# Two-layer cross-attention: the first layer's bias column computed for two batches at once, its averages over partitions in one rounded product of four columns

## What is computed

```python
q = Wq y + bq; k = Wk y + bk; v = Wv x + bv        # 1x1 convolutions over channels, 8 heads of 16 channels
scores = q k^T / sqrt(128)                          # per head, channel by channel: 16 x 16, summed over L = 1024
out = softmax(scores) v
o = Wo out + bo + x
o_hat = (o - mean(o)) * rsqrt(var(o) + 1e-5)        # mean and variance over channels and L of a batch
h = o_hat * gn_w + gn_b
```

## Time and profile before

| | |
|---|---|
| median of 3 runs | 1253.28 us |
| profiled execution, device time | 1253.11 us |
| its span | 1251.3 us |
| TensorE matmul busy | 1239.6 us, 99% |
| TensorE weight load busy | 968.7 us, 77% |
| VectorE busy | 843.2 us, 67% |
| ScalarE busy | 807.7 us, 65% |
| GpSimd busy | 295.0 us, 24% |

### The profile page before, as it was taken

The page is one execution under the profiler, slowest core; times in us unless marked ns, Lnnn a source line. Parts: engine busy times, 40 slices in busy tenths (PEclk is TensorE's granted clock), DMA queues, the critical chain, the costliest instruction groups (busy, mean ns, idle before and its releaser), DMA issues.

```text
span 1251.3 us, 24584 instructions
## 1 busy us (share of the span) xinstructions
PE 1239.6 (99%) x7860; PEld 968.7 (77%) x7860; DVE 843.2 (67%) x1953; ACT 807.7 (65%) x2884; POOL 295.0 (24%) x297
## 2 busy tenths in 40 slices
PE   8999999999999999999999999999999999999999
PEld 6788888888887888888878877677776767677677
DVE  6777777777747767767667776776665677766554
ACT  6676776666617887887577877655555577755441
POOL 4444443222233233233333305100000111000000
PEclk9999999999999999999999999999999999999999
DMA  9689899999755445554555559998788999888872
GB/s 329 230 289 290 284 289 336 308 309 311 271 189 167 152 152 175 178 172 152 169 166 181 177 177 333 284 270 239 234 243 236 270 255 257 234 225 244 235 222 85
DMA packets 196590, 291.49 MB, mean 233 GB/s; under 512 B 14160, under 2 KB 119888, under 8 KB 195760
## 3 DMA queue, kind: packets, MB, share of 16 engines
q1 hardware_dynamic: 196464, 289.92, 74.5%
HBM read 183.96 MB, written 105.91 MB: 232 GB/s over the span
## 4 chain that ended last, share of the span: by engine, by line
PE 93%; DVE 4%; issue 1%; DMA 1%; SPq 0%; ACT 0%; DVEq 0%
PE bank L695 28%; PE bank L728 23%; PE bank L573 14%; PE bank L759 5%; PE bank L812 5%; PE bank L795 5%; PE bank L645 3%; PE bank L558 2%; PE bank L663 2%; DMA lora_raw_q<-in_factors_q 1%; PE bank L678 1%; PE bank L600 1%; PE bank L617 1%; PE bank L547 1%; DVE op L1364 1%
## 5 line engine op out<-in xcount | busy, mean ns | idle before, releaser
L1032 ACT ACTIVATE bank<-bank,negs 128x128 f32<-128x128 f32 x1024 | 353.9, 360 | 119.4 <-DVE negs L1314 118.5
L695 PE MATMUL bank<-hT,wq 128*128 128x512 f32 x1488 | 363.8, 396 | 0.0
L728 PE MATMUL bank<-wo,op 128*128 128x512 f32 (+1 forms) x1356 | 346.1, 393 | 2.0 <-DVE h_blk L1408 1.5
L695 PEld LDWEIGHTS bank<-hT,wq 128*128 128x128 f32 x1488 | 273.4, 188 | 60.8
L728 PEld LDWEIGHTS bank<-wo,op 128*128 128x128 f32 x1356 | 252.0, 188 | 62.9 <-issue 6.2
L1053 ACT ACTIVATE probT<-bank 128x512 f32<-128x512 f32 x256 | 152.6, 606 | 169.1 <-PE bank L795 166.5
L1309 DVE TENSOR_REDUCE maxes<-bank 128x4 f32<-128x512 f32 x256 | 175.1, 684 | 94.0 <-PE bank L759 93.6
L1032 ACT ACTIVATION_READ_ACCUMULATOR bank<-bank,negs 128x1 f32 x1024 | 231.3, 226 | 0.0
L573 PE MATMUL bank<-wkv_hi,yT 128*128 128x512 f32 x512 | 198.1, 415 | 0.7 <-POOL wkv_lo L1579 0.5
L1408 DVE TENSOR_TENSOR h_blk<-bank,h_blk 128x512 f32<-128x512 f32 x111 | 76.3, 687 | 95.5 <-PE bank L728 94.6
L573 PEld LDWEIGHTS bank<-wkv_hi,yT 128*128 128x128 f32 x512 | 96.5, 188 | 19.3 <-issue 1.7
(11 more groups left out here) (148 smaller groups left out, 1659.5 us busy)
## 6 DMA issues: line engine op xcount, KB each, us to landing
q_dram<-q_part SPq DMA_DIRECT2D x96, 512.0 KB, 5.7
q_stack<-q_dram SPq DMA_DIRECT2D x128, 384.0 KB, 4.8
yT_in<-in_ctx_turned SPq DMA_DIRECT2D x32, 512.0 KB, 4.9
y_in<-in_ctx SPq DMA_DIRECT2D x32, 512.0 KB, 7.1
x_in<-in_x SPq DMA_DIRECT2D x32, 512.0 KB, 5.9
h_dram<-h_out SPq DMA_DIRECT2D x32, 512.0 KB, 7.4
h_in<-h_dram SPq DMA_DIRECT2D x32, 512.0 KB, 4.0
h_blk<-h_dram SPq DMA_DIRECT2D x64, 256.0 KB, 5.2
```

What stands on the lines that cost most here:

```text
L695: m = pe.matmul(bank(u % 2).rearrange("p (a n) -> p a n", a=2), wq[:, block, part, c, :], hT[(group + 1) % 2][:, :, of, c, :], start=c == ...
L728: mm = pe.matmul(place[:, columns], op_of(pair, m)[:, of, c, :], wo[m][w][:, c, columns], start=fresh and c == 0 and of == 0 and w == 0, s ...
L1032: act.activation(part, part, ACT.Exp, bias=negs[:, n % NEGS, j:j + 1], scale=SCORE1, accum_out=sums[:, score_column(k), g, j:j + 1]).then_ ...
```

## The change

The repeated value bias becomes a third 128-column block of `first` and its column goes. The product `n1^T bv` is computed as `Wo (att bv)`: VectorE multiplies `att` by the repeated bias and sums along the row (`weigh_bias`), giving one column of `att_bv` for each batch; in odd chunks one product `woT0` x two columns (`bias_product`, ahead of `kv` chunk 5) makes both, and one VectorE operation adds `bo` to both (`add_bias`, within `partition_stats` of batch b - 1, b odd). In odd chunks `weigh_bias` comes right after the softmax, in even ones after `add_mix`; `mix_product` loses its second product. The averages: `st` and `st2` are split into upper part and rest (`split_stats`, four columns, at the end of `partition_stats`), TensorE averages the four columns with a rounded matrix of 1/128 in one product, which now comes after `kv` chunk 6, and VectorE adds upper and rest (`sum_stats`, after the second half of `yT`) ahead of `norm_factors` and `deviation`, which read that. `var_product` stays a plain fp32 product.

```diff
-        first = sb("first", [P, 6 * P + 5])
+        first = sb("first", [P, 7 * P + 4])
...
                 pe.wait_ge(S["const"], CONST["stats"])
-                pe.wait_ge(S["st"], b + 1)
-                pe.wait_ge(S["st2"], b)
-                pe.matmul(ps[:, 0:2], ones_avg[:], both_st, start=True, stop=True).then_inc(S["st1_mm"], 1)
+                pe.wait_ge(S["st_lo"], b + 1)
+                pe.matmul(ps[:, 0:4], ones_avg[:], st_split[:].rearrange("p a n -> p (a n)"), start=True,
+                          stop=True).then_inc(S["st1_mm"], 1)
...
                 pe.wait_ge(S["n1"], b + 1)
-                pe.matmul(ps[:, 0:P], wv0[:], n1[:], start=True, stop=True)
-                pe.matmul(ps[:, P:P + 1], n1[:], bv_col, start=True, stop=True).then_inc(S["mix_mm"], 1)
+                pe.matmul(ps[:, 0:P], wv0[:], n1[:], start=True, stop=True).then_inc(S["mix_mm"], 1)
+
+            def bias_product(b):
+
+                ps = small_bank("xbias", b)
+                pe.wait_ge(S["att_bv"], b + 1)
+                pe.matmul(ps[:, 0:2], woT0, att_bv[:], start=True, stop=True).then_inc(S["xbias_mm"], 1)
...
                 n1_product(b)
+                if b % 2:
+                    bias_product(b)
                 kv_products(b, (5,))
...
                 mix_product(b)
+                kv_products(b, (6,))
                 stats_product(b - 1)
-                kv_products(b, (6,))
...
+            def weigh_bias(b):
+
+                dve.wait_ge(S["att"], b + 1)
+                dve.scalar_tensor_tensor(att_bias[:], att[:], 1.0, bias_rows[:, 2, :], ALU.mult, ALU.mult,
+                                         accum_out=att_bv[:, b % 2:b % 2 + 1]).then_inc(S["att_bv"], 1)
+
+            def add_bias(b):
+                dve.wait_ge(S["xbias_mm"], b // 2 + 1)
+                dve.tensor_scalar(xbias_pair, small["xbias", b][:, 0:2], bo_col, None, ALU.add).then_inc(S["xbias"], 1)
+
             def partition_stats(b):
-                dve.wait_ge(S["xbias"], b + 1)
                 dve.wait_ge(S["mx_mm"], b + 1)
...
                 dve.bn_aggr(mv, bn[:].rearrange("p a b -> p (a b)")).then_inc(S["agg"], 1)
+                if b % 2 == 0:
+                    add_bias(b + 1)
+                dve.wait_ge(S["xbias"], b // 2 + 1)
                 dve.wait_ge(S["agg"], b + 1)
                 dve.tensor_scalar(st, mv[:, 0:1], xbias[b % 2], None, ALU.add).then_inc(S["st"], 1)
+                split_stats(b)
+
+            def split_stats(b):
+                dve.wait_ge(S["st"], b + 1)
+                if b:
+                    dve.wait_ge(S["st2"], b)
+                    dve.wait_ge(S["st1_mm"], b)
+                dve.tensor_scalar(st_split[:, 0, :], both_st, 1.0, None, ALU.mult).then_inc(S["st_hi"], 1)
+                dve.wait_ge(S["st_hi"], b + 1)
+                dve.tensor_tensor(st_split[:, 1, :], both_st, f32(st_split[:, 0, :]), ALU.subtract).then_inc(S["st_lo"], 1)
+
+            def sum_stats(b):
+                dve.wait_ge(S["st1_mm"], b + 1)
+                if b:
+                    dve.wait_ge(S["nm"], b)
+                dve.tensor_reduce(stat_sums[:], small["st", b][:, 0:4].rearrange("p (a n) -> p n a", a=2), AX_X,
+                                  ALU.add).then_inc(S["st_sum"], 1)
...
             softmax0_end(0)
+            weigh_bias(0)
             prep_lower(7)
...
                 softmax0_end(b)
+                if b % 2:
+                    weigh_bias(b)
...
                 add_mix(b)
+                if b % 2 == 0:
+                    weigh_bias(b)
                 rest_yT(b + 1, 1)
+                sum_stats(b - 1)
```

More of the change, by code:

```diff
@@ L101, in xattn_two_layers @@
         factor_tiles(lora, "lora", F32R, "kv", "o")
-        ones_avg = sb("ones_avg", [P, P])
-        first = sb("first", [P, 6 * P + 5])
-        w0T, wv0, bqk = first[:, 0:3 * P], first[:, 3 * P:4 * P], first[:, 4 * P:6 * P].rearrange("p (a n) -> p a n", a=2)
+        ones_avg = sb("ones_avg", [P, P], F32R)
+        first = sb("first", [P, 7 * P + 4])
+        w0T, wv0, bias_rows = first[:, 0:3 * P], first[:, 3 * P:4 * P], first[:, 4 * P:7 * P].rearrange("p (a n) -> p a n", a=3)
         score_bias = sb("score_bias", [P, P])
-        bq_col, bv_col, bo_col, gnw_col, gnb_col = (first[:, 6 * P + i:6 * P + i + 1] for i in range(5))
+        bq_col, bo_col, gnw_col, gnb_col = (first[:, 7 * P + i:7 * P + i + 1] for i in range(4))
         bq_scaled = sb("bq_scaled", [P, 1])
@@ L225, in xattn_two_layers @@
             "s_mm", "s_sb", "s_max", "s_neg", "s_exp", "s_rec", "att", "n1_mm", "n1", "mix_mm",
-            "mix", "mix_hi", "mix_lo", "xbias", "x_hi", "x_lo", "mx_mm", "bn", "agg", "st",
+            "mix", "mix_hi", "mix_lo", "att_bv", "xbias_mm", "xbias", "x_hi", "x_lo", "mx_mm", "bn", "agg", "st", "st_hi", "st_lo", "st_sum",
             "st1_mm", "dev", "nm", "st2", "st2_mm", "ve", "pow", "gsc", "gbi", "h", "kv_mm",
@@ L294, in xattn_two_layers @@
                 use_small(7, ("prep", unit_of(b - 1)), ("prep_merged", unit_of(b - 1) + 1))
-            for name, done in (("gram", "gram"), ("t1", "t1"), ("s", "s_sb"), ("n1", "n1"), ("mix", "xbias")):
+            for name, done in (("gram", "gram"), ("t1", "t1"), ("s", "s_sb"), ("n1", "n1"), ("mix", "mix")):
                 use_small(6, (name, b), (done, b + 1))
+            if b % 2:
+                use_small(7, ("xbias", b), ("xbias", b // 2 + 1))
             if b:
-                use_small(7, ("st", b - 1), ("nm", b))
+                use_small(7, ("st", b - 1), ("st_sum", b))
             if b - 1 >= LATE_STATS:
@@ L593, in var_product @@
                 pe.wait_ge(S["st2"], b + 1)
-                pe.matmul(ps[:, 0:1], ones_avg[:], st2, start=True, stop=True).then_inc(S["st2_mm"], 1)
+                pe.matmul(ps[:, 0:1], f32(ones_avg[:]), st2, start=True, stop=True).then_inc(S["st2_mm"], 1)
             def t1_product(b):
@@ L1205, in norm_factors @@
                 if b < LATE_STATS:
-                    dve.wait_ge(S["st1_mm"], b + 2)
-                    var = small["st", b + 1][:, 1:2]
+                    dve.wait_ge(S["st_sum"], b + 2)
+                    var = stat_sums[:, 1:2]
                 else:
@@ L1429, in vector_program @@
             dve.wait_ge(S["bq_scaled"], 1)
[L1430 removed]
+            dve.scalar_tensor_tensor(score_bias[:], bias_rows[:, 1, :], bq_scaled[:], score_bias[:],
                                      ALU.mult, ALU.add).then_inc(S["score_bias"], 1)
@@ L1497, in vector_program @@
                 if w == 2:
+                    sum_stats(B - 1)
                     deviation(B - 1)
```

24 lines of the change are left out of this document (14 added, 10 removed).

## The result

The changed kernel takes 1259.12 us (median of 4 runs, 1257.0 to 1259.75), the kernel before beside it 1253.19 (4 runs, 1252.61 to 1253.95): ratio 1.0039, 95% interval 1.0027 to 1.0051. It is 5.9 us slower; 1.1 us above the upper end of the range, where no change was forecast. The profiled execution took 1259.19 with a span of 1257.4.

What follows compares the result with a forecast made beforehand. TensorE was taken as the bound, with VectorE's 0.87 us slack before `yT` spent by the change. Terms -1.0 + 0.96 + 0.28 + 0.75 = +1.0 on 1253.11 gave 1254.3 us, no discernible change; own range 1251 to 1256.5, 8-in-10 range 1249 to 1258.

Steps and rivals of the forecast that it cites:

- The steady pair, 20.19: Chunks 2 to 29: an odd and an even chunk together take 20.19 us against 20.26; 14 pairs give -1.0 us.
- The signs I named: Changed profile: period alternating near 10.2 and 10.0, fifth gram product idle for `yT`, idle before VectorE's first gram addition gone.
- rival A: Steady chunks: VectorE keeps up; 1248.7 us, or about 1247 with everything TensorE saves kept; chance 0.28.
- What they feed is due a chunk later, so I count nothing.: GpSimd's `x_lo` and weight rest and SyncE's loads move by 1.1 us; counted nothing, up to 1 if a load is late.
- Chunk 31, nothing: Chunk 31 ends on a VectorE stretch that waits for GpSimd anyway, so no added time.
- Chunk 1, +0.75: Chunk 1: GpSimd's `x_lo` holds the split's subtraction and delays both `yT` halves, +0.75 us; 0 if not held.
- Chunk 30, +0.96: Chunk 30: VectorE's deviation operations come later by split, weighing and sums, so the waiting variance product costs +0.96 us.
- Chunk 0, +0.28: Chunk 0: `weigh_bias` ahead of the last lower half of `wkv`, less one bias product, and a larger `first`: +0.28 us.
- B: Chunks 2 to 29: VectorE's accumulation costs more than taken; at 0.19 a chunk 1256.8 us, slower; chance 0.27.
- C: Averages: the four-column product takes two passes, 0.11 more TensorE time a chunk; 1254.5 us, within the no-change case's 0.45.
- the +1.0 of the forecast: Whole kernel: steady chunks and edges sum to +1.0 us on the profiled execution's 1253.11.

Runs made afterwards that it cites:

- e6: Changed kernel with GpSimd's `x_lo` of batch 1 delayed until VectorE's rest of mix, and `lora_o` cut into eight pieces over chunks 2 to 9; ratio 0.9995 to the kernel before.
- e8: Kernel before the change with GpSimd's `x_lo` of batch 1 delayed and `lora_o` cut into eight pieces; ratio 0.9991 to the kernel before.
- e3: Changed kernel with the sums of the averages written to two more columns of their own PSUM bank instead of an SBUF tile; ratio 1.0017 to the kernel before.
- e11: Kernel before the change with both GpSimd moves and the variance products of chunks 30 and 31 behind `kv` chunk 7; ratio 0.9989 to the kernel before.
- e2: Changed kernel with the bias column and its product as before the change, so the averages part alone; ratio 1.0023 to the kernel before.
- e13: Changed kernel with only GpSimd's `x_lo` of batch 1 delayed, `lora_o` left in two pieces; ratio 1.0009 to the kernel before.

## Why the prediction was wrong

- **The steady pair, 20.19: measured 20.00 where it is best, 20.08 in the mean; too pessimistic.** What TensorE saves was right: from the `gram` product to the next chunk 0.32 less in even and 0.13 less in odd chunks, 0.45 a pair where 0.49 was counted. VectorE's additions were 0.15 (odd) and 0.10 (even) too large (the accumulation measured 0 instead of 0.10, and `add_bias` holds the shift up by 0.09 instead of 0.15). The signs I named came: a period alternating near 10.2 and 10.0 as 10.12 (odd) and 9.88 (even), the idle time ahead of VectorE's first gram addition gone, TensorE late for `yT`, though by 0.06 behind odd and 0.12 behind even chunks, not more in odd ones. At the mean of 0.19 a pair, 14 pairs give 2.7 instead of 1.0; with the rest of the sum as it stands that is 1252.6, still far from rival A's 1248.7.
- **"What they feed is due a chunk later, so I count nothing."** This is the step that failed, and with it the "nothing" of chunk 31 below; besides, the sum has no term for the clock. I followed GpSimd's later chain forward to its users and not sideways to what it holds off while it runs. In the changed kernel its `power`, `x_lo`, `lora_o` and weight rest of chunk 2 run to 53.72. The weight rest begins 0.06 ahead of att scaling; before, it began 1.10 ahead (49.04 against 50.14) and was 0.20 from its end, which cost att scaling nothing (0.29). The 1.1 that I had forecast for the chain was right (1.04 by these rows), and laid beside VectorE's time it gives the collision: 49.04 + 1.1 = 50.14. It costs 1.0 in chunk 3; with the second `lora_o`, att scaling takes 0.81 in chunk 6, about 0.5 of the 0.8 lost in chunks 6 and 7. e6 removed both; the rest in chunk 6 is the wait for `kv_sb`, which isn't GpSimd's.
- **The clock.** The sum prices a stall as its own length. Behind the stalls of chunks 1 and 30 the clock went to its lower level for some 3 us, 1.4 each time, 2.8 together. No single collision cost as much as one of them.
- **Chunk 1, +0.75.** The collision was foreseen, its size not. The held operation was the split's first one, `tensor_scalar` with one SBUF input, which I had not counted among those that can be held. TensorE stood 2.25 at the averages, for which this term counts no wait (0.34 before): 0.7 of it is the held split, 1.53 is VectorE's longer order and stays in e6; and the clock fell behind it. Chunks 1 and 2 together lost 1.3, although the old collision, worth 1.0 by e8 (0.26 late at chunk 1, 0.74 early at chunk 3), was gone.
- **Chunk 30, +0.96.** Right: the variance product's load waits 2.02 instead of 1.03 (the product itself 1.85 instead of 0.62), and the next gram came 0.88 later. Not counted: the clock behind it, which makes the way from there to the second stage 1.4 longer (2.50 more than before, against 1.08 in e6, whose clock held).
- **Chunk 31, nothing.** Wrong by 1.1, what e6 loses there without a clock fall: `deviation` had read the mean from PSUM and now reads it from SBUF, so GpSimd's `x_lo` can hold it (1.22 instead of 0.14 in the rows above; 0.15 in e3, with `x_lo` running). A change of the memory in which an operand lies was priced as no change.
- **Chunk 0, +0.28.** The gram of chunk 1 starts 0.97 and 0.71 later in the two profiles of the changed kernel, but 0.26 and 0.46 in e8 and e11, which have no part of the change: some 0.4 may be the difference between executions, and the rest is near the estimate; no run separates them.
- **Rivals.** A's outer figure doesn't add up: 1253.1 - 6.9 + 2.0 for the edges is 1248.2, not 1247. B had the sign by the wrong mechanism; the accumulator costs nothing. C is refuted: one averaging load, at 197.84, and the next load 0.11 later. The Trainium skill's rule, "VectorE: DVE Perf Modes", section "Two Vector instructions with no wait between them", that an accumulating operation is two instructions, is seen in the trace; its second part takes 0.08, but the next operation starts with it, so 0.00 didn't fall away as the low end.

Sum by the gram starts: 0.97 in chunk 0, 1.3 in 1 and 2, 1.0 in 3, 0.8 in 6 and 7, 3.4 in 30 and 31, less 2.1 in the steady chunks and 0.1 in 4 and 5, is 5.2 of the 6.1 between the spans. The last 0.9 is in the second stage, which wasn't touched; no run separates it from the difference between executions. Against the +1.0 of the forecast, the terms that it lacked are the clock (2.8) and GpSimd's holds in chunks 3, 6 and 31 (2.6); what the steady chunks gave beyond the forecast took 1.1 off again.

## What to carry to other kernels

When a chain on GpSimd moves, lay its new times beside VectorE's and look for operations with all operands in SBUF, the small ones too: a subtraction of one column can be held until GpSimd's instruction ends. Price a stall of TensorE like those here (1.5 to 2.3 us) with the clock that may fall behind it, 1.4 us each time that it fell here, which no idle time shows. And try a part of a change in the order that the change gives it: its place was worth 10 us here, the part itself about 1.

## What was not expected of the hardware

- A held operation of 128x2 elements took 0.90 (changed kernel) and 1.84 (e2) against 0.17, one of 128x1 1.22 against 0.15.
- Filler products of 0.22 us each, put in front of a wait, kept the clock at 1.00 and were worth 2.0 us, although those of chunk 30 delayed the product behind them by 0.9.
- The same stall of chunk 30 (1.84 to 1.87) was followed by a clock fall in three profiles (the changed kernel's two, e3) and not in two others (e6, e13); one of 1.47 was (e2), and one of 2.22 in chunk 1 was not (e2).
